# Four sub-layers on one Trainium2 core: where the low pass of an output product stands among TensorE's transposes

## Chip, cores and metric

The kernel runs on one core of one Trainium2 chip. The metric is the device time of one execution in microseconds (us), given as the median of three runs. All arithmetic is in f32 or in pairs of f32 values of reduced precision (fp32r): a number is split into a high part and a low part, and a product is made of three passes, high times high, high times low and low times high.

## The reference

`x` has 2 batches of 1024 rows of 256 numbers. Four sub-layers follow one another, each on a layer norm of `x` and each added to `x`:

```python
x = x + _L0_xattn_ref(_layernorm(x), ctx_768, ...)  # 16 heads over 64 keys, then relu(out @ W1 + b1) @ W2 + b2
x = x + _L0_ffn_ref(_layernorm(x), ...)             # 8 low-rank experts on a shared FFN 256 -> 1024 -> 256, top-2 gates
x = x + _L1_xattn_ref(_layernorm(x), ctx_768, ctx_768, ...)   # one head, 64 keys
x = x + _L1_ffn_ref(_layernorm(x), ...)             # x @ weight.T + pooled(x) @ disha
```

## The kernel before

The 2048 rows are cut into 8 blocks (`NBLK`) of `T = 256` rows, and each block into `NT = 2` tiles of 128 rows. The work on one block is long and is spread over a software pipeline. After an opening for blocks 0 and 1 come seven bodies, `i = 1` to `7`, and then a drain and an end. The opening counts as the first body in the name of the change, so that its "third body" is `i = 2`. Body `i` works on four blocks at once:

- `a = i`: the attention of the first sub-layer, its two products (`a_hidden`, `a_out`), and the second norm
- `f = i - 1`: the FFN with the experts (`f_base`, `f_first`, `f_second`, `f_out`)
- `c = i - 2` (missing in body 1): the third and fourth sub-layer (`c_scores`, `c_transpose`, `c_attend`)
- `h = i + 1` (missing in body 7): the queries and the row maxima of the next attention

The order on each engine is the order in which the code is written, in one function `body` per engine. Engines wait for one another by counting semaphores. The names that matter here, on TensorE unless another engine is named:

- `f_out(f, t, high, low)` is the output product of the FFN for tile `t`, out of `hid_h` and `hid_l` (the parts of the hidden values, 8 chunks) and `wo`, into half `t` of one PSUM bank, `I_(0)`. With `high` it issues 16 matmuls on `hid_h`, with `low` the 8 on `hid_l` (the low pass). The last low pass of tile 1 signals `x2_ps`.
- `hid_l` is written by GpSimd (line 1779), four instructions to a block.
- `a_max_transposes(h)` (line 423) turns the row maxima `mx`. It is kept back by the semaphores `mx`, `x1` and, by the line ahead of it, `z`.
- `transposes(2, a, T_(1))` (line 362) turns the second norm's result `xn` for the block: two transposes for each tile, each pair behind `ln2_xh`, which ScalarE signals when it has written the tile (line 967).
- ScalarE then copies the turned block out of PSUM as `xtf_h` (line 972), VectorE makes `xtf_l` from it (line 1286), and `f_gate` (line 347, `ga`) multiplies both with the gate weights.
- `second_residual(f)` on VectorE (line 1420) waits for `x2_ps` and writes `x2`. It stands behind `low(2, ...)`, the instruction that makes `xtf_l`.
- `c_turn(f)` (line 605) waits for `x2` and turns it. Out of it come `xtc_h` (ScalarE, line 972) and `xtc_l` (VectorE, line 1286), for which `c_scores` of the next body waits.

The two places on VectorE and TensorE that set one another's order are these:

```python
                if A_:
                    low(2, a, XTF, T_(1))
...
                if F_:
                    second_residual(f)
                    dve.wait_ge(S("x2"), (f + 1) * NT)
                    statistics(3, f, X2)
                if A_:
                    experts(a)
```

Of the kernel before, what the change touches and what calls it, by code (L numbers as in the profile page):

```python
# [62 lines left out]
def build(nc, io):  # L63
# [173 lines left out]
    with block:  # L237
# [91 lines left out]
        def _(pe):  # L329
# [12 lines left out]
            def passes(parts, chunks, pairs, start, stop):  # L342

                for a, b in pairs:
                    for i, (out, lhs, rhs) in enumerate(parts):
                        for k, c in enumerate(chunks):
                            last = mm(out, lhs(a, c), rhs(b, c), start=start and (a, b) == pairs[0] and i == 0 and k == 0,  # L347
                                      stop=stop and k == len(chunks) - 1, skip_group_check=True)
                return last

            def w(name, m, n=P):

                return lambda a, c: (WH, WL)[a][name][:, c, m:m + n]

            def x_of(halves, lo=0, n=T):
                return lambda a, c: halves[a][:, c, lo:lo + n]

            def transposes(j, b, bank):
                for t in range(NT):
                    pe.wait_ge(S(f"ln{j}_xh"), b * NT + t + 1)  # L360
                    for c in range(KC):
                        last = nc.tensor.transpose(bank[:, c * T + t * P:c * T + (t + 1) * P],  # L362
                                                   XN[j][:, t, c * P:(c + 1) * P], ident)
                last.then_inc(S(f"ln{j}_T"), 1)
# [55 lines left out]
            def a_max_transposes(b):  # L420
                pe.wait_ge(S("mx"), (b + 1) * NT)
                pe.wait_ge(S("x1"), b)
                nc.tensor.transpose(P_(1)[0:NT * MXW, 0:P], mx[:, :], ident).then_inc(S("mxT_ps"), 1)
# [37 lines left out]
            def a_scores(b, d):  # L461

                if b == 1 and d == 1:
                    pe.wait_ge(S("crow"), 2)
                if d == 0:
                    if b == 1 or b == BPB:
                        pe.wait_ge(S(f"ks{b // BPB}"), 16 * 3)
                        pe.wait_ge(S("tables"), b // BPB + 1)
                    for r in range(3):
                        pe.wait_ge(S(f"qstack{r}"), b * 16 * GPC)  # L470
                    pe.wait_ge(S("mstack"), (b + 1) * NT)
                if d >= 2:
                    pe.wait_ge(S("ex"), b * DPAIRS + d - 1)
                for k in range(2):
                    last = mm(S_(d % 2)[:, k * T:(k + 1) * T], KS[:, b // BPB * PAIRS + 2 * d + k, :],  # L475
                              QS[:, 2 * d + k, :], start=True, stop=True)
                last.then_inc(S("sc"), 1)
# [62 lines left out]
            def f_lora_transposes(b):  # L540
                pe.wait_ge(S("am"), b + 1)
                for k in range(2 * NT):
                    last = nc.tensor.transpose(P_(0)[:, k * P:(k + 1) * P], am[:, k * P:(k + 1) * P], ident)
                last.then_inc(S("amT"), 1)
# [26 lines left out]
            def f_first(b, u, bank=None):  # L571
                if u == 0:
                    if b == 0:
                        pe.wait_ge(S("lo_wp"), 3)
                    pe.wait_ge(S("atl"), b + 1)
                f_lora(b, u, 0, "first_ps", bank)

            def f_second(b, u, bank=None):

                pe.wait_ge(S("r1"), b * NDF + u + 1)  # L580
                f_lora(b, u, 1, "second_ps", bank)

            def f_out(b, t, high=True, low=True):

                if t == 0:
                    if b == 0:
                        pe.wait_ge(S("lo_wp"), 5)
                    pe.wait_ge(S("hidh"), (b + 1) * NDF)
                part = [(I_(0)[:, t * D:(t + 1) * D], x_of((HH, HL), t * P, P), w("wo", 0, D))]
                if high:  # L590
                    passes(part, range(NFF), ((0, 0), (0, 1)), t == 0, False)
                if low:
                    pe.wait_ge(S("hidl"), (b + 1) * NDF)
                    last = passes(part, range(NFF), ((1, 0),), False, True)
                    if t == NT - 1:
                        last.then_inc(S("x2_ps"), 1)
# [15 lines left out]
            def c_scores(b, t):  # L612

                if t == 0:
                    if b == 0:
                        pe.wait_ge(S("gw_l"), 1)
                    split_in(3, b)
                three(T_(t)[:, 0:SY], x_of(XTC, t * P, P), folded_weights(b), range(KC)).then_inc(S("sc1_ps"), 1)

            def c_transpose(b):  # L620

                pe.wait_ge(S("y"), (b + 1) * NT)
                pe.wait_ge(S("ex1"), b + 1)
                nc.tensor.transpose(T_(1)[:, 0:P], sc1[:, :], ident).then_inc(S("ex1T"), 1)
# [21 lines left out]
            def fold_means():  # L646

                pe.wait_ge(S("consts"), 1)
                pe.wait_ge(S("wc_sum"), 1)
                for c in range(KC):  # L650
                    last = mm(T_(1)[:, 0:GW], avg[:, 0:1].broadcast_to([P, P]), GWR[:, c, :], start=c == 0,
                              stop=c == KC - 1)
                last.then_inc(S("gw_mean"), 1)
# [155 lines left out]
            def body(a, f, c, h):  # L809
                A_, F_, C_, H_ = (v is not None for v in (a, f, c, h))  # L810
                if A_:
                    a_scores(a, 0)
                    a_scores(a, 1)
                if F_:
                    f_lora_transposes(f)
                if f == 0:
                    fold_means()
                if C_:
                    c_scores(c, 0)
                    c_scores(c, 1)  # L820
                if F_:
                    f_first(f, 0)
                    if A_:
                        a_scores(a, 2)
                    f_first(f, 1)
                    if A_:
                        a_scores(a, 3)
                    f_second(f, 0)
                    if A_:
                        a_attend(a)  # L830
                    f_second(f, 1)
                    if C_:
                        c_transpose(c)
                    f_base(f, 2)
                    f_first(f, 2)
                    if C_:
                        c_attend(c)
                    f_base(f, 3)
                if F_:
                    f_second(f, 2)  # L840
                    f_first(f, 3)
                if C_ and H_:
                    a_queries(h)
                if f == 0:
                    pe.wait_ge(S("gw"), 1)
                    transposes(1, h, T_(1))
                    fold_values()
                if A_:
                    a_hidden(a, 0)
                if A_:  # L850
                    a_hidden(a, 1)
                if H_ and not C_:
                    a_queries(h)
                if F_:
                    f_second(f, 3)
                if A_:
                    a_out(a, 0)
                if H_ and not C_:
                    a_row_scores(h, 0)
                elif H_:  # L860
                    row_scores(h)
                if A_:
                    a_out(a, 1)
                if F_:
                    f_out(f, 0, low=False)
                if H_ and not C_:
                    a_row_scores(h, 1)
                if F_:
                    f_out(f, 1, low=False)
                if C_:  # L870
                    pe.wait_ge(S("z"), (c + 1) * NT)
                if H_:
                    a_max_transposes(h)
                if A_:
                    transposes(2, a, T_(1))
                if F_:
                    f_out(f, 0, high=False)
                    f_out(f, 1, high=False)
                if A_:
                    f_gate(a, h)  # L880
                    if F_:
                        if f == 0:
                            pe.wait_ge(S("vv_l"), 2)
                        c_turn(f)
                    f_base(a, 0)
                    f_base(a, 1)
                elif F_:
                    c_turn(f)
# [1117 lines left out]
```

## Time and profile before

| | us |
|---|---|
| median of 3 runs | 313.53 (313.51 to 314.56) |
| the profiled execution, whole | 311.67 |
| its span in the profile | 309.8 |
| TensorE busy with matmuls | 294.8 |
| TensorE's weight loads busy | 271.4 |
| VectorE busy | 257.4 |
| ScalarE busy | 172.5 |
| GpSimd busy | 161.0 |

PE is TensorE, PEld its weight loads, DVE is VectorE, ACT is ScalarE and POOL is GpSimd. A time in the trace counts from the span's start. The ends of matmuls are modelled, so the distance from one start to the next says more than a duration. The profiled execution lies 1.86 us under the median of the timed runs, and 1.87 us of it lie around its span.

### The profile page before, as it was taken

The numbers are of one execution on the slowest core, as the hardware profiler recorded it, in microseconds if no ns is written. First come the engines' busy times: TensorE is split into PE (matmuls) and PEld (weight loads), VectorE is DVE, ScalarE is ACT, GpSimd is POOL, SyncE is SP. The second block draws the span as 40 slices with busy tenths as digits, with TensorE's granted clock in tenths as the row PEclk, the third lists the DMA queues.
The fourth block names the chain that finished last, engine by engine and source line by source line (L and its number), as shares of the span: only waits on it lengthen the run. The fifth ranks groups of instructions, "written<-read, shape, count | busy, mean of one in ns | idle before, by whom it ended". The sixth has DMA issues, their size and how long they took to land.

```text
span 309.8 us, 6696 instructions
## 1 busy us (share of the span) xinstructions
PE 294.8 (95%) x2548; PEld 271.4 (88%) x2548; DVE 257.4 (83%) x706; ACT 172.5 (56%) x359; POOL 161.0 (52%) x156
## 2 busy tenths in 40 slices
PE   7789998999999999999999999999999999999972
PEld 5559788999989998999999998999899998999971
DVE  3898888979899889998799889988999879756666
ACT  3558387655657357635845565735763584434521
POOL 1946665893176606590467218660659044803562
PEclk9999999999999999999999999999999999999996
DMA  7993320023022310133013200231113100000000
GB/s 238 397 376 103 89 51 2 0 56 115 2 21 51 92 63 10 26 89 103 2 19 85 87 35 19 51 98 56 6 26 93 36 0 2 0 34 3 2 34 34
DMA packets 15904, 20.18 MB, mean 65 GB/s; under 512 B 2913, under 2 KB 11873, under 8 KB 15617
## 3 DMA queue, kind: packets, MB, share of 16 engines
q1 hardware_dynamic: 14176, 16.19, 19.1%
q10 hardware_dynamic: 1696, 3.57, 3.2%
q8 instruction: 20, 0.33, 0.5%
q14 instruction: 12, 0.09, 0.2%
HBM read 11.62 MB, written 2.63 MB: 46 GB/s over the span
## 4 chain that ended last, share of the span: by engine, by line
PE 62%; DVE 22%; ACT 5%; issue 4%; POOL 3%; DMA 2%; SPq 0%; DVEq 0%; POOLq 0%
PE psI L338 12%; PE psI L567 12%; PE psP L347 8%; PE psI L347 4%; PE psT L338 4%; DVE st L1271 3%; ACT xn L967 3%; PE psP L502 2%; PE psS L347 2%; DMA kv<-in_kv 2%; PE psS L475 2%; POOL rs L1756 2%; DVE mx L1321 2%; PE psT L634 2%; PE psT L362 2%
## 5 line engine op out<-in xcount | busy, mean ns | idle before, releaser
L1756 POOL TENSOR_TENSOR rs<-ve,mhalf 128x2 f32<-128x2 f32 x30 | 22.0, 734 | 88.7 <-DVE ve L1282 88.7
L1779 POOL TENSOR_TENSOR hid_l<-r,hid_h 128x512 fp32r<-128x512 f32 x32 | 40.9, 1291 | 16.0 <-ACT hid_h L1046 16.0
L567 PE MATMUL psI<-at_h,lb_h 128*128 128x256 f32 x120 | 34.6, 288 | 0.8 <-DVE at_l L1404 0.8
L567 PE MATMUL psI<-at_h,lb_l 128*128 128x256 f32 x120 | 33.8, 282 | 0.0
L567 PE MATMUL psI<-at_l,lb_h 128*128 128x256 f32 x120 | 33.6, 280 | 0.0
L1412 DVE SCALAR_TENSOR_TENSOR r<-psI,nbi,r 128x256 f32<-128x256 f32 x60 | 26.1, 476 | 6.4 <-PE psI L567 6.4
L1773 POOL TENSOR_TENSOR hs_l<-hs,hs_h 128x512 fp32r<-128x512 f32 x15 | 19.6, 1311 | 20.5 <-ACT hs_h L1026 19.6
L967 ACT ACTIVATE xn<-xmid,nmr,rs 128x256 f32<-128x256 f32 x16 | 8.7, 593 | 35.8 <-POOL nmr L1760 35.8
L1041 ACT ACTIVATE r<-psI,first 128x256 f32<-128x256 f32 x60 | 25.1, 472 | 4.3 <-PE psI L567 4.3
L567 PEld LDWEIGHTS psI<-at_h,lb_h 128*128 128x128 f32 x120 | 22.6, 188 | 4.3 <-ACT r L1041 2.9
L1046 ACT ACTIVATE hid_h<-r 128x512 fp32r<-128x512 f32 x32 | 19.9, 627 | 11.0 <-DVE r L1412 11.0
L338 PE MATMUL psI<-xtf_h,wi_h 128*128 128x256 f32 x120 | 25.9, 297 | 0.0
L338 PE MATMUL psI<-xtf_h,wi_l 128*128 128x256 f32 x120 | 24.1, 282 | 0.0
L338 PE MATMUL psI<-xtf_l,wi_h 128*128 128x256 f32 x120 | 23.9, 281 | 0.0
L1005 ACT ACTIVATE ex<-psS 128x512 f32<-128x512 f32 x28 | 15.9, 599 | 14.2 <-PE psS L475 14.2
L567 PEld LDWEIGHTS psI<-at_h,lb_l 128*128 128x128 f32 x120 | 22.6, 189 | 0.0
L567 PEld LDWEIGHTS psI<-at_l,lb_h 128*128 128x128 f32 x120 | 22.6, 188 | 0.0
L338 PEld LDWEIGHTS psI<-xtf_h,wi_h 128*128 128x128 f32 x120 | 18.3, 189 | 2.2 <-issue 2.2
L338 PEld LDWEIGHTS psI<-xtf_l,wi_h 128*128 128x128 f32 x120 | 18.4, 188 | 0.0
L338 PEld LDWEIGHTS psI<-xtf_h,wi_l 128*128 128x128 f32 x120 | 18.4, 188 | 0.0
L1015 ACT ACTIVATE oa_h<-o 128x256 fp32r<-128x256 f32 x16 | 6.7, 418 | 18.2 <-DVE o L1355 17.3
L1764 POOL TENSOR_TENSOR oa_l<-o,oa_h 128x256 fp32r<-128x256 f32 x15 | 11.9, 814 | 9.4 <-ACT oa_h L1015 9.4
(344 smaller groups left out, 910.7 us busy)
## 6 DMA issues: line engine op xcount, KB each, us to landing
stack<-qu_h SPq DMA_DIRECT2D x56, 64.0 KB, 2.1
xin<-in_x SPq DMA_DIRECT2D x8, 256.0 KB, 2.7
stack<-qu_l SPq DMA_DIRECT2D x28, 64.0 KB, 2.0
out<-x ACTq DMA_DIRECT2D x7, 256.0 KB, 2.0
xn<-in_xt SPq DMA_DIRECT2D x5, 256.0 KB, 2.9
raw_w<-in_w ACTq DMA_DIRECT2D x2, 512.0 KB, 8.0
raw_wi<-in_wi SPq DMA_DIRECT2D x1, 1024.0 KB, 9.3
raw_wo<-in_wo SPq DMA_DIRECT2D x1, 1024.0 KB, 11.9
```

The source lines that it names most:

```text
L338: last = mm(out, lhs(a, c), rhs(b, c), start=start and q == 0 and k == 0, stop=stop and q == 2 and k == n - 1, **kw)
L347: last = mm(out, lhs(a, c), rhs(b, c), start=start and (a, b) == pairs[0] and i == 0 and k == 0, stop=stop and k == len(chunks) - 1, skip_ ...
L567: last = mm(bank[:, k * T:(k + 1) * T], (WH, WL)[x]["lb"][:, 0, f * P:(f + 1) * P], AT[y][:, which, :], start=False, stop=q == 2, skip_gro ...
L967: A(XN[j][:, t, :], src[:, t, :], ACT.Identity, scale=lnst[j][4][:, t:t + 1], bias=lnst[j][5][:, t:t + 1]).then_inc(S(f"ln{j}_xh"), 1)
L1005: A(EX[:, 2 * d:2 * d + 2, :], S_(d % 2).rearrange("p (k n) -> p k n", k=2), ACT.Exp, scale=SCALE).then_inc(S("ex"), 1)
L1041: last = A(R1[:, f, :], bank[:, k * T:(k + 1) * T], ACT.Relu, bias=cols[:, BI + f:BI + f + 1])
L1046: A(HH[:, 2 * u:2 * u + 2, :], R1[:, 2 * u:2 * u + 2, :], ACT.Identity).then_inc(S("hidh"), 1)
L1412: last = V.scalar_tensor_tensor(out=R1[:, f, :], in0=bank[:, k * T:(k + 1) * T], scalar=nbi[:, f:f + 1], in1=R1[:, f, :], op0=MAX, op1=ADD)
L1756: G_.tensor_tensor(rs[:, :], ve[:, :], mhalf[:, :], ALU.pow).then_inc(S(f"ln{j}_rs"), 1)
L1764: G_.tensor_tensor(OA[1][:, m, :], O32[:, m, :], as32(OA[0][:, m, :]), ALU.subtract).then_inc(S("ol"), 1)
L1773: G_.tensor_tensor(HS[1][:, two, :], HS32[:, two, :], as32(HS[0][:, two, :]), ALU.subtract).then_inc(S("hsl"), 1)
L1779: G_.tensor_tensor(HL[:, two, :], R1[:, two, :], as32(HH[:, two, :]), ALU.subtract).then_inc(S("hidl"), 1)
```

## The change

In each body that has a block `c` (`i = 2` to `7`), the low pass of tile 0 of the output product is issued ahead of the wait for `z`, of the turned maxima and of the second norm's transposes, instead of behind them. The low pass of tile 1 stays where it was. In body 1 nothing moves. No instruction is added or taken away, and only TensorE's order changes.

```diff
@@ -867,14 +867,17 @@
                     a_row_scores(h, 1)
                 if F_:
                     f_out(f, 1, low=False)
+                if F_ and C_:
+                    f_out(f, 0, high=False)
                 if C_:
                     pe.wait_ge(S("z"), (c + 1) * NT)
                 if H_:
                     a_max_transposes(h)
                 if A_:
                     transposes(2, a, T_(1))
+                if F_ and not C_:
+                    f_out(f, 0, high=False)
                 if F_:
-                    f_out(f, 0, high=False)
                     f_out(f, 1, high=False)
                 if A_:
                     f_gate(a, h)
```

On TensorE, in each of the bodies 2 to 6, the order changes at this place (`psI<-wo_h,hid_l` is the low pass, `psP<-first,mx` the turned maxima, `psT<-first,xn` the second norm's transposes):

```order
 L347 MATMUL psI<-wo_h,hid_h 128x256 x8
 L347 MATMUL psI<-wo_l,hid_h 128x256 x8
+L347 MATMUL psI<-wo_h,hid_l 128x256 x8
 L423 MATMUL psP<-first,mx 64x128
 L362 MATMUL psT<-first,xn 128x128 x4
-L347 MATMUL psI<-wo_h,hid_l 128x256 x16
+L347 MATMUL psI<-wo_h,hid_l 128x256 x8
 L347 MATMUL psP<-ga_h,xtf_h 128x136 x4
 L347 MATMUL psP<-ga_l,xtf_h 128x136 x4
```

Eight of the sixteen low matmuls have moved up past five transposes.

On TensorE in body 7, which has no block `h` and so no turned maxima, with the semaphores that each instruction waits for:

```order
-L362 MATMUL psT<-first,xn 128x128 [waits ln2_xh,z]
-L362 MATMUL psT<-first,xn 128x128
-L362 MATMUL psT<-first,xn 128x128 [waits ln2_xh]
-L362 MATMUL psT<-first,xn 128x128
 L347 MATMUL psI<-wo_h,hid_l 128x256 [waits hidl,hidh]
 L347 MATMUL psI<-wo_h,hid_l 128x256 x7
+L362 MATMUL psT<-first,xn 128x128 [waits ln2_xh,z]
+L362 MATMUL psT<-first,xn 128x128
+L362 MATMUL psT<-first,xn 128x128 [waits ln2_xh]
+L362 MATMUL psT<-first,xn 128x128
```

The four transposes have moved behind the first eight low matmuls, which wait for GpSimd's `hidl` and no longer stand behind `ln2_xh`.

## Rows read from the trace of the kernel before

**Rows 1.** The page: span, TensorE's and its loads' busy time, granted clock

```profile
span 309.8 us, 6696 instructions
...
PE 294.8 (95%) x2548; PEld 271.4 (88%) x2548; DVE 257.4 (83%) x706; ACT 172.5 (56%) x359; POOL 161.0 (52%) x156
...
PEclk9999999999999999999999999999999999999996
```

**Rows 2.** Chain that ended last, in body 6: start, us, what

```profile
204.47 0.70 POOL rs L1756
...
205.47 1.10 ACT xn L967 x2
206.58 0.04 issue
206.62 0.44 PE psT L362 x2
207.06 1.90 PE psI L347 x16
```

**Rows 3.** Instructions of L362: what TensorE sat idle for, in us and times

```profile
  ACT xn L967: 4.7, 16
```

**Rows 4.** Timeline, TensorE's weight loads: body 3's place, then body 6's

```profile
105.53 0.20 PEld L362 LDWEIGHTS psT<-first,xn 128*128 128x128 f32 x2 [0.38 <-ACT xn L967]
...
205.66 0.11 PEld L423 LDWEIGHTS psP<-first,mx 128*64 128x64 f32 x1
206.12 0.20 PEld L362 LDWEIGHTS psT<-first,xn 128*128 128x128 f32 x2 [0.36 <-ACT xn L967]
206.62 0.20 PEld L362 LDWEIGHTS psT<-first,xn 128*128 128x128 f32 x2 [0.29 <-ACT xn L967]
...
208.68 0.53 PEld L347 LDWEIGHTS psP<-ga_h,xtf_h 128*128 128x128 f32 x4
...
210.05 0.42 PEld L605 LDWEIGHTS psT<-first,x 128*128 128x128 f32 x4
...
214.21 0.30 PEld L338 LDWEIGHTS psT<-gw_h,xtc_h 128*128 128x128 f32 x2
```

**Rows 5.** Timeline, TensorE's matmuls in body 6

```profile
204.80 1.12 PE L347 MATMUL psI<-wo_l,hid_h 128*128 128x256 f32 x8
205.76 0.27 PE L423 MATMUL psP<-first,mx 128*64 128x128 f32 x1
...
206.81 2.15 PE L347 MATMUL psI<-wo_h,hid_l 128*128 128x256 f32 x16
208.80 0.56 PE L347 MATMUL psP<-ga_h,xtf_h 128*128 128x136 f32 x4
...
210.09 0.62 PE L605 MATMUL psT<-first,x 128*128 128x128 f32 x4
210.47 0.48 PE L338 MATMUL psI<-xtf_h,wi_h 128*128 128x256 f32 x2
```

**Rows 6.** Timeline, the other engines at the same place in body 6

```profile
201.44 2.53 POOL L1779 TENSOR_TENSOR hid_l<-r,hid_h 128x512 fp32r<-128x512 f32 x2
...
207.09 0.60 ACT L972 ACTIVATE xtf_h<-psT 128x512 fp32r<-128x512 f32 x1 [0.53 <-PE psT L362]
...
207.73 0.69 DVE L1286 TENSOR_TENSOR xtf_l<-psT,xtf_h 128x512 fp32r<-128x512 f32 x1 [0.38 <-ACT xtf_h L972]
...
209.00 0.88 DVE L1420 SCALAR_TENSOR_TENSOR x<-psI,gate,xg 128x256 f32<-128x256 f32 x2 [0.58 <-PE psI L347]
...
212.98 0.42 DVE L1389 TENSOR_TENSOR am<-am 128x256 f32<-128x256 f32 x1
213.32 0.68 DVE L1286 TENSOR_TENSOR xtc_l<-psT,xtc_h 128x512 fp32r<-128x512 f32 x1
```

**Rows 7.** Timeline of body 7: matmuls, loads and VectorE

```profile
270.81 1.12 PE L347 MATMUL psI<-wo_l,hid_h 128*128 128x256 f32 x8
272.75 2.15 PE L347 MATMUL psI<-wo_h,hid_l 128*128 128x256 f32 x16
...
274.94 0.88 DVE L1420 SCALAR_TENSOR_TENSOR x<-psI,gate,xg 128x256 f32<-128x256 f32 x2 [0.58 <-PE psI L347]
...
280.00 0.30 PEld L338 LDWEIGHTS psT<-gw_h,xtc_h 128*128 128x128 f32 x2 [0.18 <-DVE xtc_l L1286]
```

## The prediction

> **What bounds the kernel now.** The page comes first. TensorE is busy for 294.8 us of a span of 309.8 us, at the full granted clock in all tenths but the last [rows 1]. With 95% of the span taken by one engine, a change can only pay where this engine stands still, or where it sets what comes late to it.
>
> The chain of work that ended last is read next, because it shows which of two engines' work ends a wait. In body 6 it does not run through TensorE up to the place of the change. It comes from GpSimd's inverse root of the second norm, runs through ScalarE's two `xn` instructions, and goes over to TensorE only with the second pair of transposes; from there on it is TensorE's own low pass [rows 2]. So TensorE arrives at the transposes before their input does. The reader is to see the change of engine at 206.62.
>
> How long TensorE stands still there is in the view of line 362: its loads sat idle for 4.7 us in all until ScalarE's `xn` came, in 16 waits [rows 3]. In body 6 the two pairs wait 0.36 and 0.29 us, and in body 3 the first pair waits 0.38 [rows 4], so the pattern repeats itself. The idle figure of the loads also holds some distance that would be there without a wait. The stall is better read from the starts of matmuls. From the turned maxima at 205.76 to the first low matmul at 206.81 there are 1.05 us for five transposes [rows 5]. Four transposes without a wait take 210.47 - 210.09 = 0.38 us, or 0.095 each [rows 5], so five would take 0.48. **The stall is 1.05 - 0.48 = 0.57 us in each body.**
>
> **The work that moves.** Eight matmuls of the low pass have the same shape as the eight before the turned maxima, which take 205.76 - 204.80 = 0.96 us [rows 5]. They need `hid_l`, which GpSimd finished at 201.44 + 2.53 = 203.97 [rows 6]. That is 1.7 us before TensorE's load at 205.66 [rows 4], so the move brings no wait for GpSimd. Nothing else is added: the waits are the same in number, and no other engine's order is touched.
>
> The new order in body 6, with times counted as before: low pass of tile 0 from 205.76 to 206.72, then the turned maxima, then the four transposes from 206.82, and the low pass of tile 1 from 207.20. `xn` was complete at 205.47 + 1.10 = 206.57 [rows 2], so the first pair, whose load is issued at about 206.71, and the second, 0.2 us later, no longer wait. TensorE by itself has won the full 0.57 us at this point.
>
> **What is late next.** The transposes, though, now end later than they did. A last transpose ends 0.24 us after the start of the next matmul: 0.62 us from 210.09 is 210.71, against 210.47 [rows 5]. That gives 207.44, where the chain shows 207.06 before [rows 2]. What hangs on them is 0.38 us later:
>
> - ScalarE's `xtf_h` ends at 207.09 + 0.60 + 0.38 = 208.07. The gate product's first load stood at 208.68 [rows 4] and would now stand at 208.68 - 0.57 = 208.11. With the 0.04 us that the chain shows between engines [rows 2] this just fits, so I take no stall.
> - VectorE's `xtf_l` starts at 207.73 + 0.38 = 208.11 [rows 6]. Behind it stands the second residual, which before started at 209.00 after 0.58 us of idle time for the low pass [rows 6]. TensorE would now be done with that at about 208.33, so VectorE is the one to go by. An instruction that follows without a wait starts some 0.08 us before the end shown of the one ahead (212.98 + 0.42 = 213.40 against 213.32 [rows 6]). The residual starts at 208.11 + 0.69 - 0.08 = 208.72, which is 0.28 us earlier than before, and ends at 209.60.
> - `c_turn` needs `x2`. Its first load stood at 210.05 [rows 4]. TensorE alone would bring it to 210.05 - 0.57 = 209.48, but `x2` allows it at 209.60 + 0.04 = 209.64. So 0.16 of the 0.57 us is given back, and 210.05 - 209.64 = **0.41 us stays in each body.**
> - The next meeting is `c_scores`. Its load would come to 214.21 - 0.41 = 213.80 [rows 4]. `xtc_l` ended at 213.32 + 0.68 = 214.00 [rows 6] and moves with VectorE by 0.28 to 213.72, or 213.76 with the way over. It fits by 0.04 us. The operand `am` of the transposes ahead of it was done at 213.40 and moves in the same way, with more room.
>
> The rest of a body starts from events of TensorE and moves with it: I found no wait there that hangs on work of the other engines from ahead of the place. So I carry the 0.41 us through, as five times for the bodies 2 to 6: 2.05 us.
>
> Body 7 has no turned maxima. TensorE is free at 270.81 + 0.96 = 271.77, and the first low matmul came at 272.75 [rows 7]: 0.98 us for four transposes of 0.38, a stall of 0.60. Here `c_scores` waited for `xtc_l` before, by 0.18 us of idle loads [rows 7], so only VectorE's shift counts. Transposes from 272.73 end at 273.11 + 0.24 = 273.35, against 272.99 before (272.75 + 0.24), 0.36 later. In body 6 a delay of 0.38 made the residual 0.28 us earlier, out of a slack of 0.66; a delay of 0.36 out of much the same slack leaves **0.30 us**.
>
> **The sum** is 2.05 + 0.30 = 2.35 us. Against the profiled execution, 311.67 becomes 309.3 and the span 307.4 to 307.5. The median of the runs shown lies 1.86 us above that execution; I take the same difference off it: 313.53 - 2.35 = **311.2 us**, or 0.75% less.
>
> **The costs from both sides.** The 0.41 us rests on the price of a transpose behind matmuls and on the way through ScalarE and VectorE, which the trace does not show in this order. If VectorE's path lay free, the stall of TensorE would go whole: 0.57 us five times and 0.60 once make 3.45 us. On the other side, each 0.1 us by which the transposes end later takes 0.1 us off in each body. In the trace the first matmul after a wait can come a good 0.1 us late (the pairs at 206.12 and 206.62 stand 0.5 us apart); with two such steps of 0.1 us the gain is 0.21 in each of five bodies and 0.10 in the last, 1.15 us. I stay at 0.41, since in the new order nothing in the row of transposes waits.
>
> The four transposes are priced by the row above, at 0.095 us each. The Trainium skill, TensorE: Matmul & The Clock Gate, section "Back-to-back issue gap", gives some 81 ns for each in a sustained stream of loads and matmuls of 128 columns. By that the five would cost 0.41 us and not 0.48, the transposes would end 0.07 us earlier, and the gain would be some 0.4 us more in all. This case's rows at 0.095 us speak against it, and the sum goes by them.
>
> **The rivals.**
>
> 1. *TensorE alone counts* (10%). The stall goes and nothing takes its place: 313.53 - 3.45 = 310.1 us. For it speaks that VectorE had 0.58 us of idle time at the place; against it that the part after the transposes adds up to more than that slack leaves.
> 2. *Most of it turns into a new wait* (15%). `xtf_h`, `x2` and `xtc_l` each fit or miss by less than 0.2 us. If the way from the transposes to `x2` is 0.2 us longer than I have it, as above, 1.15 us is left: 312.4 us.
> 3. *It does nothing* (7%). If the transposes' input moved with TensorE's order, or if a median of three runs hides the change, the time stays at 313.5 us. Against it: the second norm's chain starts from `x1_ps`, which is ahead of everything that moves.
> 4. *Slower: VectorE's slack is overdrawn* (7%). The eight matmuls cost 0.96 us ahead of the transposes. Only what TensorE stood still pays for them. If the transposes came the whole 0.96 us later instead of 0.38, `xtf_l` would push the second residual, which has 0.66 us of room (208.34, the earliest start behind `xtf_l`, to 209.00), 0.30 us past its place. `c_turn` and `c_scores` would follow, six times: 1.8 us, so 315.3 us. It decides from a delay of 0.66 us on. Against it: the wait of 0.57 us is in three rows and is gone by construction once `xn` is there first.
>
> **How the numbers follow.** My forecast has 61%, and its own range is 310.7 to 312.0 us (a gain of 0.27 to 0.50 us in a body). The range for 8 times in 10 reaches from rival 1 at 310.0 to a part of rival 2 and the scatter of a median, 312.8; what is left out above is rivals 3 and 4 and the edge of rival 2. Faster by over 0.5% (some 1.6 us, about what can be told from no change here) are my forecast and rival 1, less the forecast's edge: 69%. Within 0.5% are rivals 2 and 3 and that edge: 24%. Slower is rival 4: 7%.
>
> **What the profile after would show.** The idle time of line 362 for `xn` falls from 4.7 us to under 1. The distance from the turned maxima to the next low matmul falls from 1.05 to about 0.5 us. The idle time of 0.58 us ahead of VectorE's second residual is gone, and a new wait of `c_turn` for `x2` of about 0.15 us appears. The period of a body falls by 0.4 us. The prediction is wrong if the loads of the gate product wait for `xtf_h` by more than 0.1 us, if `c_turn`'s new wait is over 0.3 us, or if `c_scores` waits for `xtc_l` in the bodies 2 to 6 as well.

## The result, and the profile after

The changed kernel's median is 311.79 us over 22 runs, beside 314.64 us for the kernel before on the same chips. The ratio is 0.9918, with a 95% interval of 0.9895 to 0.9941: 0.82% faster, where 0.75% was forecast. The executions fall into a faster and a slower state, and every ratio here is taken over the faster ones alone, so that it is not the quotient of the medians; the traces too are of such executions, but for the one with sixteen ahead, which is of a slower one, and the one with the change in body 4 alone, whose state is not known. In absolute terms 311.2 us were forecast, from a median of 313.53 us before. The larger sample has a median before that is 1.1 us higher; less the 2.35 us of the forecast it would give 312.3, so the measured 311.79 lies between the two. The profiled execution took 309.51 us with a span of 307.5 us, and 311.67 and 309.8 before [rows 1]. The page of the changed kernel:

```profile
span 307.5 us, 6696 instructions
...
PE 293.0 (95%) x2548; PEld 272.3 (89%) x2548; DVE 256.8 (84%) x706; ACT 172.6 (56%) x359; POOL 161.2 (52%) x156
...
PEclk9999999999999999999999999999999999999997
...
PE 83%; DVE 8%; ACT 3%; DMA 2%; issue 2%; POOL 1%; SPq 0%; POOLq 0%; DVEq 0%
```

The clock is as before. The last line is the share of each engine in the chain that ended last. Now 83% of the span are TensorE's own work, where it was 62% in the kernel before:

```profile
PE 62%; DVE 22%; ACT 5%; issue 4%; POOL 3%; DMA 2%; SPq 0%; DVEq 0%; POOLq 0%
```

One thing about the numbers of the bodies. In the trace before, the turned maxima start at 38.96 us in the opening and at 71.82, 105.15, 138.70, 172.24, 205.76 and 239.31 us in the bodies `i = 1` to `6`. The place at 205.76 us, which the rows and the prediction call body 6, is therefore body 5 by `i`, and the one at 105.53 us, called body 3, is body 2. From here on bodies are numbered by `i`. The sum does not change by it, since the place looks the same in the bodies 2 to 6. The chain in body 5 shows where the share comes from; these rows answer to [rows 2] (start, us, what):

```profile
201.15 4.80 PE psI L347 x40
205.95 0.11 PE psP L423
206.06 0.44 PE psT L362 x4
206.50 0.95 PE psI L347 x8
207.45 1.35 PE psP L347 x12
208.80 0.55 PE psT L605 x4
```

ScalarE's `xn` and GpSimd's inverse root are gone from the chain, and TensorE goes from the output product over the maxima and all four transposes without a break that this view shows. The instructions of line 362 give the same in one row, which answers to [rows 3]:

```profile
  ACT xn L970: 1.1, 4
```

The 4.7 us of 16 waits are 1.1 us of 4; none of them is in the bodies 2 to 7. Two, 0.50 us, are in body 1, which was not changed, and two are in the opening. The timeline of the place in body 5, all engines, answers to [rows 4 to 6]:

```profile
204.83 1.12 PE L347 MATMUL psI<-wo_h,hid_l 128*128 128x256 f32 x8
...
205.79 0.27 PE L423 MATMUL psP<-first,mx 128*64 128x128 f32 x1
...
205.90 0.60 PE L362 MATMUL psT<-first,xn 128*128 128x128 f32 x4
...
206.22 1.02 PEld L347 LDWEIGHTS psI<-wo_h,hid_l 128*128 128x128 f32 x8
206.25 1.20 PE L347 MATMUL psI<-wo_h,hid_l 128*128 128x256 f32 x8
206.53 0.60 ACT L975 ACTIVATE xtf_h<-psT 128x512 fp32r<-128x512 f32 x1 [0.90 <-PE psT L362]
...
207.16 0.69 DVE L1289 TENSOR_TENSOR xtf_l<-psT,xtf_h 128x512 fp32r<-128x512 f32 x1 [0.73 <-ACT xtf_h L975]
207.24 0.52 PEld L347 LDWEIGHTS psP<-ga_h,xtf_h 128*128 128x128 f32 x4
...
207.77 0.87 DVE L1423 SCALAR_TENSOR_TENSOR x<-psI,gate,xg 128x256 f32<-128x256 f32 x2
...
208.69 0.42 PEld L605 LDWEIGHTS psT<-first,x 128*128 128x128 f32 x4
```

Three things are to be seen. The way from the turned maxima to the next low matmul is 206.25 - 205.79 = 0.46 us, where it was 1.05. VectorE's second residual follows `xtf_l` without idle time, where it had waited 0.58 us for TensorE. And from the start of the place to `c_turn`'s load there are 208.69 - 204.83 = 3.86 us, where there were 210.05 - 205.76 = 4.29: 0.43 us less.

### The profile page after: what moved, and what is told of

The parts are those of the page before. It is cut to its first block, busy times and chain, and to the rows that moved or that the text cites. A ratio compares the mean times of both kernels' runs of the same rounds, so it can differ in the third digit from the quotient of the medians.

```text
span 307.5 us, 6696 instructions
## 1 busy us (share of the span) xinstructions
PE 293.0 (95%) x2548; PEld 272.3 (89%) x2548; DVE 256.8 (84%) x706; ACT 172.6 (56%) x359; POOL 161.2 (52%) x156
## 4 chain that ended last, share of the span: by engine, by line
PE 83%; DVE 8%; ACT 3%; DMA 2%; issue 2%; POOL 1%; SPq 0%; POOLq 0%; DVEq 0%
PE psI L567 13%; PE psP L347 13%; PE psI L338 12%; PE psI L347 12%; PE psS L347 7%; PE psT L338 4%; PE psP L502 2%; DMA kv<-in_kv 2%; PE psS L475 2%; PE psT L634 2%; PE psT L362 2%; PE psP L742 1%; PE psT L605 1%; PE psP L543 1%; ACT hs L1024 1%
```

## The experiments

Each kernel is compared by its trace in two lengths, because they resolve some 0.05 us where the ratios of whole runs have intervals that are 0.5 to 1.4% wide. The first is the mean period of a body, from the turned maxima of body 2 to those of body 6, divided by four. The second is the stretch from the start of the place in body 1 (its turned maxima, or the low matmuls ahead of them) to the first matmul of `c_scores` behind body 7. The whole span is of less use here, since the opening ran at a lower granted clock in some executions. The clock rows of the kernels with five and with sixteen ahead show it among their first four slices of forty (a 9 is full or nearly so):

```profile
PEclk9799999999999999999999999999999999999996
```

```profile
PEclk9987999999999999999999999999999999999996
```

| kernel | low matmuls ahead | period, us | stretch, us | against before | ratio (95%) |
|---|---|---|---|---|---|
| before | 0 | 33.54 | 208.18 | | |
| two_ahead | 2 | 33.31 | 206.86 | -1.32 | 0.9947 (0.9906 to 0.9988) |
| five_ahead | 5 | 32.98 | 204.84 | -3.34 | 0.9881 (0.9823 to 0.9938) |
| six_ahead | 6 | 32.94 | 204.70 | -3.48 | 0.9846 (0.9776 to 0.9917) |
| the changed kernel | 8 | 33.12 | 205.70 | -2.48 | 0.9918 (0.9895 to 0.9941) |
| after_again | 8 | 33.14 | 205.80 | -2.38 | 0.9849 (0.9785 to 0.9913) |
| maxima_first | 8 | 33.12 | 205.75 | -2.43 | 0.9922 (0.9891 to 0.9954) |
| sixteen_ahead | 16 | 34.09 | 211.57 | +3.39 | 1.0089 (1.0046 to 1.0132) |
| five_and_body1 | 5, and 4 in body 1 | 32.97 | 204.67 | -3.51 | 0.9886 (0.9838 to 0.9935) |
| six_vv_first | 6, and 4 in body 1 | 32.96 | 204.31 | -3.87 | 0.9886 (0.9829 to 0.9943) |

The period of the changed kernel, for example, is (238.92 - 106.44) / 4, and its stretch 277.79 - 72.09, from these rows of its matmuls (the one at 269.93 is the start of the place in body 7):

```profile
72.09 0.27 PE L423 MATMUL psP<-first,mx 128*64 128x128 f32 x1
...
106.44 0.27 PE L423 MATMUL psP<-first,mx 128*64 128x128 f32 x1
...
238.92 0.27 PE L423 MATMUL psP<-first,mx 128*64 128x128 f32 x1
...
269.93 1.11 PE L347 MATMUL psI<-wo_h,hid_l 128*128 128x256 f32 x8
...
277.79 0.56 PE L338 MATMUL psT<-gw_h,xtc_h 128*128 128x320 f32 x2
```

### How many matmuls stand ahead: two, five, six, sixteen

The theory (A below) is that of the prediction: the wait is covered up to its length, and what is put ahead beyond it makes VectorE late. Its rivals have TensorE's order alone set the gain. In the kernels with two, five and six, `f_out` takes a range of chunks for its low pass:

```diff
-                if F_ and C_:
-                    f_out(f, 0, high=False)
+                ahead = 5 if C_ else 0
+                if F_ and ahead:
+                    f_out(f, 0, high=False, low=range(ahead))
...
-                if F_ and not C_:
-                    f_out(f, 0, high=False)
                 if F_:
+                    f_out(f, 0, high=False, low=range(ahead, NFF))
                     f_out(f, 1, high=False)
```

> Two of the eight low matmuls stand ahead, six behind. Theory A: two matmuls cover 0.24 us of the stall of 0.57, the transposes still wait for xn for about 0.3 us, and nothing behind them is late, so a body takes 33.54 - 0.24 = 33.30 us and the span is some 1.4 us under the kernel before. Theory B says the same here. A third reading, in which the gain comes from anything being issued ahead of the wait (the load of the first transpose, say) and not from its length, gives 33.12 us as with eight.

> Five of tile 0's eight low matmuls stand ahead of the turned maxima and the transposes, three behind, in the bodies 2 to 7. Theory A (the eight cover the whole stall of 0.57 us, and 0.16 us is given back because the transposes, and so VectorE's xtf_l and second residual, come 0.38 us later): five matmuls are 0.60 us, just the stall, so the transposes end where they did in the kernel before. VectorE reaches the second residual in time, c_turn does not wait for x2, and a body takes 33.54 - 0.56 = 32.98 us, against 33.12 for the changed kernel; the span is 0.9 us under the changed kernel's (some 306.6 us). Theory B (the gain is set by TensorE's order alone, and what is behind the transposes does not give anything back): a body takes the same 33.12 us as with eight, or more, since less is ahead.

> Six of the eight low matmuls ahead, two behind. Theory A: 0.72 us against a stall of 0.57 delays the transposes by 0.15 us, VectorE's second residual by as much (its start 208.49 where TensorE allows 208.37), and x2 is there at 209.41, still ahead of c_turn's load at 209.48. So nothing is given back and a body takes 32.97 us, as with five; from seven on c_turn would have to wait. A theory in which every delay of the transposes costs TensorE time gives 32.98 + 0.12 = 33.10 us.

The kernel with sixteen moves both tiles' low passes:

```diff
                 if F_ and C_:
                     f_out(f, 0, high=False)
+                    f_out(f, 1, high=False)
...
                 if F_ and not C_:
                     f_out(f, 0, high=False)
-                if F_:
                     f_out(f, 1, high=False)
```

> The low passes of both tiles, sixteen matmuls or 1.92 us, stand ahead of the maxima and the transposes. Theory A: the transposes end 0.38 + 0.96 = 1.34 us later than in the kernel before, which overdraws VectorE's room of 0.66 us by 0.68: the gate product waits for xtf_h by about 1 us, c_turn for x2, and a body takes 33.54 + 0.55 = 34.1 us; the span is 3.4 us over the kernel before (313 us). Theory B (order of TensorE alone counts): the stall is covered as with eight, 33.0 to 33.1 us.

Measured were periods of 33.31, 32.98, 32.94 and 34.09 us, against 33.30, 32.98, 32.97 and 34.1 expected. Two matmuls pay for what they take, so length is what counts. Five and six win more than eight, which no theory of TensorE's order alone allows. Between five and six the traces do not decide (0.04 us), and seven, from which on `c_turn` was expected to wait, was not run. Sixteen are slower than none, and the ratio of 1.0089 says so too (some 2.8 us of 314.57). Its span was 319.3 us and not the 313 expected, again for an opening that was longer, by 6 us. The span of the run with five was 308.2 us and not the 306.6 expected, because its opening was longer as well (the turned maxima of body 1 stood at 73.58 us, against 72.09 in the changed kernel); its stretch is 0.86 us shorter than the changed kernel's, as expected. The place in body 5 with five ahead:

```profile
205.92 0.76 PE L347 MATMUL psI<-wo_h,hid_l 128*128 128x256 f32 x5
...
206.63 0.60 PE L362 MATMUL psT<-first,xn 128*128 128x128 f32 x4
...
207.89 0.69 DVE L1290 TENSOR_TENSOR xtf_l<-psT,xtf_h 128x512 fp32r<-128x512 f32 x1 [0.37 <-ACT xtf_h L976]
208.26 0.53 PEld L347 LDWEIGHTS psP<-ga_h,xtf_h 128*128 128x128 f32 x4
...
208.58 0.88 DVE L1424 SCALAR_TENSOR_TENSOR x<-psI,gate,xg 128x256 f32<-128x256 f32 x2
...
209.63 0.42 PEld L606 LDWEIGHTS psT<-first,x 128*128 128x128 f32 x4
```

From the gate product's first load to `c_turn`'s load there are 209.63 - 208.26 = 1.37 us, exactly as before the change (210.05 - 208.68 [rows 4]). With eight ahead it is 208.69 - 207.24 = 1.45 us. That 0.08 us is the wait for `x2`: the second residual ends at 207.77 + 0.87 = 208.64, 0.05 us ahead of `c_turn`'s load, where with five ahead it ends 0.17 us ahead of it. With sixteen ahead, at the same place, the loads wait for `xtf_h` first:

```profile
216.27 0.60 ACT L975 ACTIVATE xtf_h<-psT 128x512 fp32r<-128x512 f32 x1 [1.86 <-PE psT L362]
216.90 0.69 DVE L1289 TENSOR_TENSOR xtf_l<-psT,xtf_h 128x512 fp32r<-128x512 f32 x1 [1.68 <-ACT xtf_h L975]
216.98 0.52 PEld L347 LDWEIGHTS psP<-ga_h,xtf_h 128*128 128x128 f32 x4 [0.99 <-issue]
217.01 0.64 PE L347 MATMUL psP<-ga_h,xtf_h 128*128 128x136 f32 x4 [0.78 <-ACT xtf_h L975]
...
217.50 0.87 DVE L1423 SCALAR_TENSOR_TENSOR x<-psI,gate,xg 128x256 f32<-128x256 f32 x2
218.43 0.42 PEld L605 LDWEIGHTS psT<-first,x 128*128 128x128 f32 x4
```

0.99 us of idle loads are more than the stall of 0.57 us that was won. With the 0.08 us at `c_turn` (218.43 - 216.98 = 1.45, as with eight) this leaves a loss of 0.50, and the period is 0.55 us longer.

### Is it the maxima or the transposes that were late?

```diff
-                if F_ and C_:
-                    f_out(f, 0, high=False)
                 if C_:
                     pe.wait_ge(S("z"), (c + 1) * NT)
                 if H_:
                     a_max_transposes(h)
+                if F_ and C_:
+                    f_out(f, 0, high=False)
...
```

> As the changed kernel, but the wait for z and the turned maxima stand ahead of the low pass of tile 0 again; only the four transposes stay behind it. Theory A: the maxima were ready (mx at 205.52 us of the kernel before), only xn was late, so a body takes 33.12 us as in the changed kernel and the span is the same within 0.3 us. The rival, that part of the gain came from giving the row maxima or z more time, makes it longer by that part, up to 0.4 us in each body.

The period is 33.12 us, the same as with the change as it was made. The span of 307.0 us is 0.5 us under the changed kernel's, where at most 0.3 was expected; the turned maxima of body 1 stand 0.55 us earlier (71.54 against 72.09), so this difference too lies in the opening. The maxima and `z` had nothing to win. The whole gain comes from moving work past the wait for `xn`.

### One body alone, and the changed kernel again

In this kernel the condition is `a == 4` in place of `C_`.

> The change in body 4 alone, all other bodies as in the kernel before. Theory A: nothing is carried from body to body, since every chain starts anew at an event of TensorE, so the stretch from the turned maxima of body 3 to those of body 5 is shorter by the 0.42 us of one body in all and the others take 33.54 us; the gain of the change is a sum of bodies. If a body's gain needed its neighbours' (or if its neighbours lost by it), the stretch would differ by 0.2 us or more from that.

From the maxima of body 3 at 145.38 to those of body 5 at 212.10 there are 66.72 us, against 205.76 - 138.70 = 67.06: 0.34 less, not 0.42. The body with the change is as long as it should be. Its place starts at 178.97 and the next at 212.10, 33.13 us. Of the missing 0.08 us, 0.05 are in the unchanged body 3 ahead of it, which took 178.97 - 145.38 = 33.59 us, and in this execution body 2 already took 145.38 - 111.80 = 33.58 us. Both lie ahead of the place that was changed. So a body's gain does not need its neighbours', and 0.05 us of such a length is scatter between executions. The one execution of this kernel took 318.07 us in all, with the turned maxima of body 1 at 78.46 us; by whole times nothing could have been told.

```profile
145.38 0.27 PE L423 MATMUL psP<-first,mx 128*64 128x128 f32 x1
...
178.97 1.12 PE L347 MATMUL psI<-wo_h,hid_l 128*128 128x256 f32 x8
...
212.10 0.27 PE L423 MATMUL psP<-first,mx 128*64 128x128 f32 x1
```

> The changed kernel once more, beside the others on the same chip: a body of 33.12 us and a ratio to the kernel before of 0.992.

The period came out at 33.14 us. The ratio was 0.9849 (0.9785 to 0.9913), which overlaps the 0.9918 of the larger sample. Two samples of the same kernel 0.7% apart show that the ratios here cannot rank the kernels with five, six and eight ahead. The traces can.

### Body 1, and who takes its gain back

```diff
-                ahead = 5 if C_ else 0
+                ahead = 5 if C_ else 4
```

> Five matmuls ahead in the bodies 2 to 7 as in the run with five, and four ahead in body 1 too, where the change leaves the old order. In body 1 the turned maxima stood at 71.82 us and the first low matmul at 72.68 before (0.86 us, of which 0.48 are five transposes without a wait), so a stall of 0.38 us is left there. Theory A: four matmuls (0.48 us) cover it, with 0.1 us of delay for the transposes, and body 1 is 0.38 us shorter; a later body takes 32.98 us. Against the changed kernel that is 0.14 us in five bodies, about 0.2 us in body 7 and 0.38 us in body 1: 1.3 us less, or 0.4% of the time. The rival, that VectorE or GpSimd (whose work in body 1 is larger) takes the gain of body 1 back before the queries of body 2, gives 0.9 us or less.

This missed. From the place in body 1 to the place in body 2 there were 104.91 - 71.63 = 33.28 us, against 33.33 before (105.15 - 71.82): 0.05 us won of 0.38. The stretch is 1.03 us under the changed kernel's and not 1.3. The timeline of body 1 in this kernel, up to the place in body 2:

```profile
71.63 0.64 PE L347 MATMUL psI<-wo_h,hid_l 128*128 128x256 f32 x4
...
73.48 0.69 DVE L1290 TENSOR_TENSOR xtf_l<-psT,xtf_h 128x512 fp32r<-128x512 f32 x1 [0.53 <-ACT xtf_h L976]
74.09 0.68 DVE L1621 TENSOR_TENSOR vv_l<-psT,vv_h 128x512 fp32r<-128x512 f32 x1
74.69 0.87 DVE L1424 SCALAR_TENSOR_TENSOR x<-psI,gate,xg 128x256 f32<-128x256 f32 x2
...
75.70 0.63 PE L606 MATMUL psT<-first,x 128*128 128x128 f32 x4 [0.17 <-DVE x L1424]
...
104.91 0.76 PE L347 MATMUL psI<-wo_h,hid_l 128*128 128x256 f32 x5
```

In body 1 VectorE has one more instruction between `xtf_l` and the second residual, `vv_l`. VectorE had next to no idle time ahead of the residual even in the kernel before (0.58 us in the later bodies; here `vv_l` ended at 74.88 us and the residual started at 74.88), and `c_turn` waits for it as soon as TensorE is faster. From the start of the place to the residual there are 3.06 us in both kernels. The last kernel moves this instruction ahead of `xtf_l`, into 0.53 us of idle time (and has six matmuls ahead in the later bodies):

```diff
-                if A_:
-                    low(2, a, XTF, T_(1))
                 if f == 0:
                     dve.wait_ge(S("vv_h"), 2)
                     V.tensor_tensor(VV[1][:, 1:2 * BATCH:2, :], ...).then_inc(S("vv_l"), 1)
+                if A_:
+                    low(2, a, XTF, T_(1))
```

> Six matmuls ahead in the bodies 2 to 7, four in body 1, and on VectorE in body 1 the instruction that makes vv_l stands ahead of xtf_l instead of between xtf_l and the second residual. In the run with five and body 1, body 1 won only 0.05 to 0.1 us of the 0.38 expected; c_turn waited for x2, and VectorE had vv_l (0.68 us) between xtf_l and the second residual, after 0.53 us of idle time ahead of xtf_l. Theory A': it was this instruction that took the gain back. Moved into the idle time it delays xtf_l by nothing, the second residual starts 0.6 us earlier, c_turn does not wait, and the stretch from the place in body 1 to the place in body 2 takes 33.33 - 0.38 = 32.95 us against 33.28. The rival, that GpSimd's or ScalarE's work of body 1 sets its length, leaves it at 33.28. Later bodies take 32.94 us as with six. In all 3.8 us less than the kernel before, a ratio of 0.988.

```profile
73.87 0.64 PE L347 MATMUL psI<-wo_h,hid_l 128*128 128x256 f32 x4
...
75.72 0.69 DVE L1290 TENSOR_TENSOR xtf_l<-psT,xtf_h 128x512 fp32r<-128x512 f32 x1
...
76.52 0.88 DVE L1424 SCALAR_TENSOR_TENSOR x<-psI,gate,xg 128x256 f32<-128x256 f32 x2
...
77.61 0.61 PE L606 MATMUL psT<-first,x 128*128 128x128 f32 x4
...
106.78 0.88 PE L347 MATMUL psI<-wo_h,hid_l 128*128 128x256 f32 x6
```

From place to place there are now 106.78 - 73.87 = 32.91 us, and `c_turn` no longer waits. The residual starts 76.52 - 73.87 = 2.65 us after the start of the place, 0.41 us sooner, where 0.6 was expected. The gain that body 1 had withheld is there, by moving one instruction of another engine. No run moves this instruction alone, without the four matmuls, so what it would be worth by itself is not shown. This kernel's whole stretch is the shortest of all, 3.87 us under the kernel before and 1.4 us under the changed one. Its ratio of 0.9886 (0.9829 to 0.9943) is clear of 1, but its interval also holds the changed kernel's 0.9918.

## Why the prediction was right

**The stall** was priced at 0.57 us in a body. The new way over the maxima and transposes is 0.46 us, not 0.48, so the stall was 1.05 - 0.46 = 0.59. The two-matmul kernel, which won 0.23 us a body for 0.24 us put ahead, shows that it was a real stall and not an effect of how it is read.

**The transposes' price.** The four transposes now take 206.25 - 205.90 = 0.35 us, or 0.088 each, where the sum had 0.095 from `c_turn`. The Trainium skill (TensorE: Matmul & The Clock Gate, "Back-to-back issue gap") gives 81 ns for loads and matmuls of 128 columns in a steady stream. The trace lies halfway between the two.

**What is given back** was priced at 0.16 us in a body, and that is what the trace shows up to `c_turn`: 0.59 less the 0.43 us by which its load comes sooner. How it comes about was placed only half right. The prediction had all of it at `c_turn` and none at the gate product. In the trace the wait at `c_turn` is 0.08 us, and the gate product's first load comes 207.24 - 206.22 = 1.02 us after the first load of the low pass, where eight loads of this pass take 0.95 at the pitch seen with five ahead (208.26 - 206.96 over eleven): 0.07 us for `xtf_h`. The step that was too small is the way from ScalarE to TensorE. The prediction took 0.04 us for it and found that the load just fits; `xtf_h` ends at 206.53 + 0.60 = 207.13, so it is 0.11. In body 7 it is 0.05 (272.11 to 272.16). There `f_gate` has one wait less, the one for `ql`; that this makes the difference is not shown. The 0.07 us cost nothing of their own here, because `c_turn` goes by `x2`, which comes from VectorE, and would have waited that much longer.

**VectorE's second residual** was forecast 0.28 us earlier. Counted from the start of the place it is 209.00 - 205.76 = 3.24 us before and 207.77 - 204.83 = 2.94 after: 0.30 us. This is the pivot of the argument, and five, six and sixteen ahead turn on it as expected. The time at which TensorE would let the residual start was put too early by 0.1 us (208.33; 209.00 less the stall of 0.57 is 208.43), which changes nothing, since VectorE's own 208.72 decides.

**The sum** was 2.05 us for five bodies and 0.30 for body 7. Measured are 0.42 in each of the four periods from body 2 to body 6, and from the start of the place in body 2 to TensorE's arrival at the place in body 7 the five bodies take 166.62 us before (271.77 - 105.15) and 164.46 after (269.93 - 105.47): 2.16 us. Body 7, from TensorE free (271.77 before, 269.93 after) to `c_scores`, took 8.23 us before and 277.79 - 269.93 = 7.86 after: 0.37 us. Body 1 came out 0.05 us longer. The stretch over all is 2.48 us shorter against 2.35. The span was forecast as 307.4 to 307.5 us and measured as 307.5; that this fits so closely is in part luck, since the opening happened to be 0.27 us longer in the trace after (72.09 against 71.82).

**The rivals.** The first (3.45 us, VectorE's path free) did not happen with eight matmuls ahead, but its number is reached when five or six stand ahead (3.34 and 3.48). The second (1.15 us) and the third are out, by the stretch of 2.48 us and by the ratio, whose interval is 1.9 to 3.3 us of 314.64. The mechanism of the fourth, forecast as 1.8 us slower for a delay of 0.96 us, is real: with sixteen ahead `xtf_h` starts 2.66 us after the start of the place (216.27 - 213.61) instead of 1.33, a delay of 1.33 us, and the stretch is 3.4 us longer.

**Signs.** Of those named for the profile after, the idle time of line 362 was to fall under 1 us and fell to 1.1: the part of the opening and of the unchanged body 1, 1.02 of the 4.7 us before, had not been counted, and the 4.7 us were not of the loads alone (two of the 16 waits, 0.57 us, are of matmuls). The new wait of `c_turn` was to be about 0.15 us and is 0.08. The rest came as said: 0.46 us from the maxima to the next low matmul, no idle time ahead of the residual, a period shorter by 0.42. None of the three signs of being wrong is there: the gate product's load waits 0.07 us, `c_turn` 0.08, and `c_scores` of the bodies 2 to 6 shows no wait for `xtc_l` (its load comes 0.07 to 0.10 us after it).

**What the prediction did not see** is that the forecast's own arithmetic already held a better kernel. The stall is 0.57 us and the piece 0.96; five or six matmuls fill it without delaying anything that matters. With six the transposes come 0.1 us later and cost nothing, because the second residual still ends 0.13 us ahead of `c_turn`'s load (209.49 against 209.62).

## What to carry to other kernels

Work moved ahead of a wait paid here up to the length of the wait, and from there on it delayed everything that hangs on the waiting instruction, at no cost as long as the other engines had room and at full cost behind that. So cut the piece to the wait, and read the room of the next engine from its idle time before the instruction that comes back to the first. Before the same move is made in an iteration that looks alike, look for what else stands in the other engine's queue between the two. Where runs scatter by more than the effect, compare one period of the loop in the trace.

## What the runs showed that was not expected

The same period came out within 0.02 us in two executions of the changed kernel (33.12 and 33.14), while their whole times in the table's samples went from 309.12 to 315.34 us in the one and 309.43 to 316.11 in the other. What differs in the profiled executions is the opening: the turned maxima of body 1 stood at 72.09 us in one and 73.07 in the other. The granted clock tells the two apart. In the first it is 1.00, the level of 2.4 GHz, in every stretch of 4 us up to 40 us. In the second it is 0.57 from 8 to 12 us, so for most of that stretch at the lower level of 1.2 GHz, and 1.00 again behind it; in the stretch ahead of it, from 4 to 8 us, TensorE had been busy for 2.13 us, against 2.94 in the first. With sixteen ahead the maxima stood at 78.0 us, and at 78.46 in the kernel with the change in body 4 alone. Both have the same clock row, in which the third and fourth slices show 8 and 7 (with sixteen ahead 0.60 from 20 to 24 us and 0.54 from 24 to 28). In the loop all slices are 9. So what made these traces' spans differ lies in the opening and not in the loop, and goes with the granted clock there. The clock is not all of it: with sixteen ahead those 8 us hold at most 0.40 x 4 + 0.46 x 4 = 3.4 us of lost clock, as an estimate, and the maxima came 5.9 us later than with eight. What the rest is stays open.
